# ScalarE's exponentials of a step, issued ahead of its evictions instead of behind them

## The reference, cut to what matters

```python
def attention_layer(x, ctx, masks):              # layers 0, 1 and 3
    q, k, v = proj(ctx, Wq), proj(ctx, Wk), proj(ctx, Wv)   # 8 heads of 16, chunks of 64 tokens
    scores = einsum('bnqhd,bnkhd->bnhqk', q, k) / 4 + mask
    out = softmax(scores) @ v @ W_out.T + b_out             # inside each chunk
    return layernorm(out.transpose * masks + x)             # over the tokens

def neighbour_layer(points, x):                  # layer 2, points = ctx
    pd = 2 * einsum('bdn,bdm->bnm', p, p) - norms_n - norms_m
    idx = top_k(pd, 30)
    # spherical coordinates of the 30 differences, three small
    # batch-normed products, softmax over 30, weighted sum of x rows
```

## Time and profile before

| what | value |
|---|---|
| median of 3 runs | 6427.92 us (6425.65 to 6432.02) |
| profiled execution | 6420.67 us |
| its span, first to last instruction | 6418.8 us |
| busy, whole span: PE, DVE, ACT, POOL | 87%, 90%, 71%, 55% |
| first stage, about 32 to 4615 us | 768 steps |
| mean granted clock of TensorE | 0.919 |

### The profile page before, as it was taken

How to read it: one execution, slowest core, us unless ns; L and a number is a source line. 1 busy time by engine, 2 the same in 40 slices (tenths; PEclk the granted TensorE clock), 3 DMA queues, 4 the chain that set the end, 5 groups by cost and what they waited for, 6 DMA issues and landing times. The chain is left out here.

```text
span 6418.8 us, 227467 instructions
## 1 busy us (share of the span) xinstructions
PE 5554.2 (87%) x82516; PEld 3410.8 (53%) x82516; DVE 5771.8 (90%) x8140; ACT 4559.4 (71%) x17241; POOL 3506.7 (55%) x3471
## 2 busy tenths in 40 slices
PE   7988888889888888888888888888759949999999
PEld 3555555555555555455555555455423337777776
DVE  7999999999999999999999999999946687777776
ACT  7888888888888888888888888888713633333333
POOL 3466666666666666666666666666640023333332
PEclk9999999989999999999999999999869979999999
DMA  2333333333333333233333333333340023333332
GB/s 44 94 105 93 98 96 95 90 95 104 100 103 96 97 96 96 88 95 98 105 101 99 96 96 97 89 95 101 97 122 0 0 59 84 86 92 91 86 90 75
DMA packets 651349, 568.72 MB, mean 89 GB/s; under 512 B 553072, under 2 KB 574832, under 8 KB 616208
## 3 DMA queue, kind: packets, MB, share of 16 engines
q1 hardware_dynamic: 613264, 284.51, 18.9%
q10 hardware_dynamic: 36864, 268.45, 11.6%
HBM read 384.76 MB, written 67.24 MB: 70 GB/s over the span
## 5 line engine op out<-in xcount | busy, mean ns | idle before, releaser
L724 ACT ACTIVATE prob<-SC,row_max 128x64 f32<-128x64 f32 x6144 | 1841.8, 337 | 423.5 <-DVE row_max L1065 415.5
L845 POOL TENSOR_TENSOR prob<-prob,row_rec 128x512 f32<-128x512 f32 x768 | 800.6, 1042 | 1413.3 <-DVE row_rec L1073 1405.0
L724 ACT ACTIVATION_READ_ACCUMULATOR prob<-SC,row_max 128x1 f32 x6144 | 1393.1, 229 | 0.0
L1057 DVE FIND_INDEX8 nbr<-top,dist 128x8 uint16<-128x1024 f32 x1024 | 1236.2, 1220 | 0.0
L1050 DVE MAX8 top<-dist 128x8 f32<-128x1024 f32 x1024 | 1192.1, 1206 | 1.6
L1052 DVE MATCH_REPLACE8 dist<-top,dist 128x1024 f32<-128x1024 f32 x768 | 925.4, 1210 | 0.0
L588 PE MATMUL SC<-k_bd,q_t 128*64 128x256 f32 x6144 | 906.3, 419 | 0.0
L609 PE MATMUL PT<-ident,prob 128*128 128x128 f32 x3072 | 503.9, 289 | 463.6 <-ACT prob_t L731 462.8
L609 PEld LDWEIGHTS PT<-ident,prob 128*128 128x128 f32 x3072 | 374.5, 148 | 941.6 <-issue 909.9
L1721 ACT ACTIVATE dense<-DM 128x512 f32<-128x512 f32 x512 | 305.6, 597 | 745.6 <-PE DM L1680 745.0
L1829 DVE TENSOR_TENSOR d_oh_a<-lo,iota_a 128x4096 bf16<-128x4096 bf16 x256 | 583.8, 2291 | 237.8 <-PE DM L1680 237.3
(11 more groups left out here) (195 smaller groups left out, 9805.5 us busy)
## 6 DMA issues: line engine op xcount, KB each, us to landing
low_all<-low_scratch ACTq DMA_DIRECT2D x256, 1024.0 KB, 5.1
k_bd<-k_t SPq DMA_DIRECT2D x3072, 16.0 KB, 1.9
placed<-compact SPq DMA_DIRECT2D x256, 192.0 KB, 3.9
ctx<-in_ctx SPq DMA_DIRECT2D x32, 512.0 KB, 4.0
mask<-in_mask SPq DMA_DIRECT2D x32, 512.0 KB, 6.7
xb<-in_x SPq DMA_DIRECT2D x32, 512.0 KB, 3.4
x_scratch<-xb SPq DMA_DIRECT2D x32, 512.0 KB, 4.7
y_scratch<-y_b SPq DMA_DIRECT2D x32, 512.0 KB, 4.7
```

The costliest lines, as they stand in the source:

```text
L724: last = act.activation(prob[:, s % 4, g * CHUNK:(g + 1) * CHUNK], SC[:, s % 2, g * CHUNK:(g + 1) * CHUNK], ACT.Exp, bias=row_max[:, s % 2 ...
L845: pool.tensor_tensor(pr, pr, row_rec[:, r % 2, :].unsqueeze(2).to_broadcast([128, 8, CHUNK]), ALU.mult).then_inc(normed, 1)
L1057: last = dve.max_index(nbr[:, uu % BPB, t, k * 8:(k + 1) * 8], best, row)
```

## The change

In ACT's `step` the block with the exponentials is moved, whole and with its three waits, from behind the evictions to the head of the step. The evictions, and everything that stands behind the exponentials, keep their order. The other engines' streams are the same.

```diff
             def step(i, s):
                 u = s // BSTEPS
+                if real(i, s, STEPS):
+                    act.wait_ge(maxed, START + i * STEPS + s + 1)
+                    act.wait_ge(transposed, at_least(i, START + i * STEPS + s - 3, START))
+                    act.wait_ge(recip_ready, at_least(i, START + i * STEPS + s - 1, START))
+                    for g in range(8):
+                        last = act.activation(prob[:, s % 4, g * CHUNK:(g + 1) * CHUNK], SC[:, s % 2, g * CHUNK:(g + 1) * CHUNK], ACT.Exp,
+                                              bias=row_max[:, s % 2, g:g + 1], accum_out=row_sum[:, s % 2, g:g + 1])
+                    last.then_inc(exped, 1)
                 if real(i, s, STEPS) and s % BSTEPS == SQUARE_AT and real(i, u + 1, BPB):
                     square(i, u + 1, False)
...
                     act.activation(dist[:, tt % DIST_BUFS, h * HALF:(h + 1) * HALF], PD[:, :], ACT.Identity,
                                    bias=xcol[:, u, tt % NT:tt % NT + 1]).then_inc(pd_copied, 1)
-                if real(i, s, STEPS):
-                    act.wait_ge(maxed, START + i * STEPS + s + 1)
-                    act.wait_ge(transposed, at_least(i, START + i * STEPS + s - 3, START))
-                    act.wait_ge(recip_ready, at_least(i, START + i * STEPS + s - 1, START))
-                    for g in range(8):
-                        last = act.activation(prob[:, s % 4, g * CHUNK:(g + 1) * CHUNK], SC[:, s % 2, g * CHUNK:(g + 1) * CHUNK], ACT.Exp,
-                                              bias=row_max[:, s % 2, g:g + 1], accum_out=row_sum[:, s % 2, g:g + 1])
-                    last.then_inc(exped, 1)
                 r = s - LAG_T
```

## The result

The changed kernel takes 6746.97 us (median of 4 runs, 6744.29 to 6751.68) against 6429.97 us before (median of 4): ratio 1.0495, 95% interval 1.0476 to 1.0513, so 317 us or 4.9% slower. The forecast was 6710 us, range 6540 to 6810.

A forecast was written before the change was run, and what follows sets the result against it. DVE was taken to bound the attention stage. A + B + C + D = 1.6 + 1.6 + 3.9 + 1.7 = 8.8 us per batch, 282 us over 32 batches, giving 6710 us; own range 6590 to 6830, over the cases 6540 to 6810.

The forecast's parts named there:

- The bound: Attention stage: DVE works 97.4% of 4583 us, so only what moves its start times counts; at most 118 us idle.
- A: Step 7 to 8: late v eviction holds up TensorE's score product; 1.6 us of new DVE idle time per batch.
- B: Step 15 to 16: v and distances evicted behind the exponentials delay the scores; 1.6 us per batch, up to 3.0.
- C: Step 16 on TensorE: its lead is lost, so 8.21 us of work against DVE's 4.33 costs 3.9 us; low end 1.9.
- D: Steps 21 and 22: late y eviction holds the bank of step 22's v product; 1.7 us per batch, ends 0 and 4.0.
- E: Late distances, q, k and elsewhere: priced at nothing; up to 1 us per batch without the cover of GpSimd's idle time.
- Faster: Rival: earlier exponentials bring prob_t forward and DVE's waits for scores go, 80 us less, 6348 us; chance 0.07.
- No change: Rival: DVE's average 5.97 us per step hides the 2.33 us delay everywhere, 6428 us; chance 0.05.
- Only v costs: Rival: only the v waits at steps 8 and 16 cost, 3.2 us per batch, 102 us, giving 6530 us; chance 0.13.
- Half clock: Rival: TensorE's new waits keep it at 1.2 GHz, the low clock spreading; 6860 us; chance 0.09.

The follow-up runs named there:

- e6: The kernel before, with v's eviction behind the exponentials in step 7 of each batch alone; 6518.04 us, ratio 1.0140.
- e11: The changed kernel with 26 extra products on TensorE ahead of step 16's wait for v, results overwritten unread; 6753.16 us, ratio 1.0503.
- e2: The changed kernel with the y evictions back ahead of the exponentials; 6687.05 us, ratio 1.0406.
- e5: The changed kernel with the v and y evictions back ahead of the exponentials; 6544.27 us, ratio 1.0180.
- e10: The changed kernel with k, v, y and distances back ahead of the exponentials; 6417.35 us, ratio 0.9986.
- e7: The kernel before, with the prob_t eviction moved ahead of the exponentials in step 21 of each batch; 6403.67 us, ratio 0.9961.
- e9: The kernel before, with prob_t and o_t ahead of the exponentials and k behind them in step 21 of each batch; 6386.11 us, ratio 0.9935.
- e3: The kernel before, with the v evictions alone moved behind the exponentials; 6697.10 us, ratio 1.0424.
- e4: The changed kernel with extra TensorE products, 26 ahead of step 16's wait for v and 22 ahead of step 22's claim of y's bank; 6733.17 us, ratio 1.0482.

## Why the prediction was right, point by point

*The bound.* Right: 317 of the stage's 321 us are DVE's waits for scores, with its busy time 12 us up.

*A, 1.6 us at step 8:* 1.76 measured. Right, and e6 shows the mechanism alone, there with the scores at half clock (2.74 us).

*B, 1.6 us at step 16:* 2.25, inside its ends (1.6 to 3.0). The exponentials started within 0.3 us of where I had them (3.02 us after `row_max` started, 3.32 before), right behind the 1.28 us of their table load; the excess is the score product at half clock, 1.1 us longer in the batch shown. At full clock it is 1.63 (e11).

*C, 3.9 us at step 17:* 3.50 on average, 2.7 to 4.1 in all batches but the first. Right: the low clock reached into this stretch as in the earlier trace rows, over the norm product, and further in most batches (7.84 us at a mean clock of 0.83, where the batch of the earlier trace rows had 8.21). The low end of 1.9 was a little low: with the clock at full it was 2.11. I had put 2.0 us of the 8.21 down to the clock, counting the overlap of the norm product with the 4.00 us of the earlier trace rows twice; e11's stretch of 6.52 us makes it 1.7.

*D, the wait at 23 up from 2.1 to about 3.8:* from a mean of 1.69 to 3.71, by 2.0 against 1.7. That y's bank holds the v product up is right: TensorE waits 4.49 us for it, and e2 takes 1.26 us of the wait at 23 away by y's place alone. That the size came out is luck, as the steps behind it are off both ways. In the batch shown the v product starts 0.35 us ahead of `prob_t`, where I had it 0.19 us behind; v and distance product run at half clock and take 4.02 us for 2.28; and the chain from transposes to scores, which I had at half clock throughout, gets the full clock back and takes 4.32 us for 5.4.

*E, nothing:* right in the changed kernel, where all other waits, step 0 included, grew by 0.4 us per batch (0.3 to 0.9, less 0.2 at step 0). But the reason given failed: the step read "distances, q, k, elsewhere" looked at DVE's reading of `dist` and at `k_bd`, not at TensorE's claim of the one `PD` bank and of k's `PJ` bank. e5 against e10 prices that at 127 us. It did not show in the sum because it overlaps with the waits for v and y: v behind alone costs 271 us, y ahead gives back 60, distances and k cost 127, together 458 for a loss of 317, found from three different starting points. That a term priced at nothing did no harm to the sum is luck.

*Sum:* 8.8 us per batch forecast, 9.9 measured (317.2/32).

*The rivals.* Faster: the 402.2 us wait for `prob_t` did shrink, to 89.0, and it brought nothing: TensorE waits elsewhere in its order instead. e7 and e9 show that for step 23 it was `prob_t` and then `o_t`, not the exponentials, that had to come sooner. No change: out, as the short steps 8, 16 and 17 do not hide the delay. Only v costs: e3 makes 271 us of it, but not by A + B; C belongs to v as well. Half clock: it shows behind the long waits of steps 16, 22 and, in e6, 8, and at steps 16 and 17 is worth 2.0 us per batch (e11); it hardly spreads, the granted clock of the whole execution being 0.914 against 0.919.

## What to carry to other kernels

In an in-order stream, an instruction moved past others is paid for by whoever waits for what it was moved past: list those clients, and at each compare the delay with the slack of the engine that bounds the stage, in its shortest steps, not on average. Prices of late evictions found one by one do not add, since one wait covers another. What releases the busiest engine is read from its own waits: here scores, and behind them the evictions that let TensorE go on, so that the faster kernels start step 21's exponentials later.

## What the runs showed of the hardware

TensorE's granted clock was 0.50 after waits of 5.58, 4.49 and 3.78 us. After one of 1.53 us (step 8 of the changed kernel) the scores still ran at 1.00 and the products behind them at 0.52. After one of 1.82 us at the same place in e3, with one of 2.94 us and 3.1 us of work ahead of it, the scores' mask product already took 0.58 us for 0.37. So the length of the last wait alone does not tell. With products put into the 5.58 us the clock stayed 1.00, and the same scores took 1.39 us instead of 2.49.

In e11's profile, with 26 products more in TensorE's stream, the wait at its turn of the loop took 6.9 us for 3.7 and, with unchanged code there, the third stage 27 us more. e4, with these 26 and 22 more, had the 27 us without the longer turn in its profile. So the two need not have one cause, and it is not shown that the products are the cause of either; neither was traced further.
